# Scores of a quad: one addition of the bias over 512 columns and one reduction for the four maxima, in place of four fused operations

## The reference, cut to what matters

```python
q = jnp.einsum('bfd,dnh->bfnh', x, Wq) * H ** (-0.5)      # 16 heads of 64
k = jnp.einsum('btd,dnh->btnh', src, Wk)
v = jnp.einsum('btd,dnh->btnh', src, Wv)
hbias = jax.nn.relu(dist[..., None] @ Wth + bth)          # 32 hidden values for each (f, t)
qs_bias = (hbias @ Wto + bto)[..., 0]                     # one bias for each (b, f, t)
logits = jnp.einsum('btnh,bfnh->bnft', k, q)
logits = logits + bias + qs_bias[:, None]                 # the same bias for all 16 heads
w = jax.nn.softmax(logits, axis=-1)
out = jnp.einsum('bnft,btnh->bfnh', w, v)
```

## Time and profile before

| | us |
|---|---|
| median of 3 runs | 1346.33 (1345.58 to 1346.62) |
| profiled execution, its own time | 1342.64 |
| span of the profiled execution | 1340.6 |
| DVE busy | 1226.7 (92%) |
| PE busy / PEld busy | 1210.5 (90%) / 989.4 (74%) |
| ACT busy | 1062.0 (79%) |
| GpSimd busy | 852.6 (64%) |

### The profile page before, as it was taken

One profiled execution on the slowest core, in us unless ns is written; L12 is line 12 of the kernel. 1 busy time (PEld: TensorE's weight loads), 2 busy tenths in 40 slices (PEclk: granted clock), 3 DMA queues, 4 the chain that ended last, 5 costly groups with the idle time before them and its releaser, 6 DMA issues. The chain is left out here.

```text
span 1340.6 us, 36744 instructions
## 1 busy us (share of the span) xinstructions
PE 1210.5 (90%) x11184; PEld 989.4 (74%) x11184; DVE 1226.7 (92%) x4922; ACT 1062.0 (79%) x3353; POOL 852.6 (64%) x889
## 2 busy tenths in 40 slices
PE   1599999999999999999999999999999999789987
PEld 1377878787878787778777777778787878566665
DVE  5899999999999999999999999999999988579997
ACT  4588888888878888888888787878788866579887
POOL 4677777777777777777777777777777754211110
PEclk8799999999999999999999999999999999999999
DMA  6000000001100000011000000110000000000000
GB/s 189 17 1 17 2 17 2 18 17 49 35 15 4 10 10 9 10 56 43 2 17 2 17 2 17 49 43 10 17 2 25 2 2 3 1 10 13 14 16 9
DMA packets 32323, 26.69 MB, mean 20 GB/s; under 512 B 6649, under 2 KB 27009, under 8 KB 32129
## 3 DMA queue, kind: packets, MB, share of 16 engines
q1 hardware_dynamic: 32128, 24.35, 6.1%
HBM read 23.29 MB, written 1.05 MB: 18 GB/s over the span
## 5 line engine op out<-in xcount | busy, mean ns | idle before, releaser
L746 ACT ACTIVATE prob<-score,nmax 128x128 f32<-128x128 f32 x1024 | 397.0, 391 | 160.6 <-DVE nmax L941 160.6
L1341 POOL TENSOR_TENSOR prob<-prob,rinv 128x512 f32<-128x512 f32 x256 | 291.6, 1139 | 178.6 <-DVE rinv L949 178.1
L894 DVE SCALAR_TENSOR_TENSOR bias_acc<-relu_z,cst_all,bias_acc 128x512 f32<-128x512 f32 x370 | 349.2, 944 | 6.7 <-ACT relu_z L729 3.1
L729 ACT ACTIVATE relu_z<-dist_g,cst_all 128x512 f32<-128x512 f32 x386 | 295.7, 807 | 12.6 <-DMA dist_g<-in_fside_BxSxS 10.1
L941 DVE CUSTOM_DVE_ANT_0 score<-L,bias 128x128 f32<-128x128 f32 x1024 | 234.1, 281 | 2.9 <-PE L L472 1.6
L1336 POOL TENSOR_TENSOR sd<-mv,half 128x1 f32<-128x1 f32 x128 | 127.0, 992 | 120.6 <-DVE mv L963 119.4
L746 ACT ACTIVATION_READ_ACCUMULATOR prob<-score,nmax 128x1 f32 x1024 | 193.7, 189 | 0.0
L482 PE MATMUL T<-ident,prob 128*128 128x128 f32 x1024 | 160.5, 279 | 6.5 <-POOL prob L1341 4.2
L525 PE MATMUL M<-wv,ctxT_all 128*128 128x512 f32 x256 | 144.6, 647 | 18.5 <-DVE hid L1018 13.1
L496 PEld LDWEIGHTS O<-probT,v 128*64 128x64 f32 x2048 | 109.7, 136 | 59.8 <-issue 52.0
L472 PE MATMUL L<-kT,qT 64*128 64x128 f32 x2048 | 148.7, 285 | 0.0
(11 more groups left out here) (134 smaller groups left out, 2160.3 us busy)
## 6 DMA issues: line engine op xcount, KB each, us to landing
dist_g<-in_fside_BxSxS SPq DMA_DIRECT2D x16, 256.0 KB, 2.9
mask_g<-in_mask_Bx1x1xS_ff SPq DMA_DIRECT2D x16, 256.0 KB, 3.2
wk<-in_L_xattn_Wk SPq DMA_DIRECT2D x4, 512.0 KB, 3.5
wv<-in_L_xattn_Wv SPq DMA_DIRECT2D x4, 512.0 KB, 3.6
wq<-in_L_xattn_Wq SPq DMA_DIRECT2D x4, 512.0 KB, 3.7
wo<-in_L_xattn_Wo SPq DMA_DIRECT2D x4, 512.0 KB, 4.2
wf<-in_L_xattn_Wf SPq DMA_DIRECT2D x8, 256.0 KB, 2.9
xr<-in_x SPq DMA_DIRECT2D x16, 64.0 KB, 1.9
```

Of the source, the lines that this page charges most:

```text
L729: nc.scalar.activation(relu_z[:, z_slot(g, k), :], dist_g[:, :, :], ACT.Relu, bias=cst(g, C_BTH + k), scale=cst(g, C_WTH + k)).then_inc(z_ ...
L746: last = nc.scalar.activation(prob[:, c, m, :], score[:, c, m, :], ACT.Exp, bias=nmax[:, c, m:m + 1], scale=-1.0, accum_out=rsum[:, c, m:m ...
L894: vec.scalar_tensor_tensor(out=bias_acc[:, :], in0=relu_z[:, z_slot(g, k), :], scalar=weight, in1=bias_acc[:, :], op0=ALU.mult, op1=ALU.ad ...
L1341: gp.tensor_tensor(prob[:, c, :, :], prob[:, c, :, :], rinv[:, c, :].rearrange("p (m o) -> p m o", o=1).broadcast_to([P, 4, P]), ALU.mult) ...
```

## The change

`score_quad` now makes one addition over the 512 columns of the bank, with the unit's bias read four times over, raises a new semaphore `summed`, waits for it, and takes the four maxima (negated) in one reduction over `score`. `score` holds the sum itself instead of its negative, so the exponential has scale 1. PE waits for `summed` instead of `scored` before it overwrites the banks.

```diff
-                wait(pe, scored, after(g, i, 4, 2 * octet - 1))
+                wait(pe, summed, after(g, i, 4, 2 * octet - 1))
...
                     last = nc.scalar.activation(prob[:, c, m, :], score[:, c, m, :], ACT.Exp, bias=nmax[:, c, m:m + 1],
-                                                scale=-1.0, accum_out=rsum[:, c, m:m + 1])
+                                                scale=1.0, accum_out=rsum[:, c, m:m + 1])
...
-                for m in range(4):
-                    if m == 0:
-                        if i % GROUP == 0 and c == 0:
-                            dve.wait_ge(bias_done, g + i // GROUP + 1)
-
-                        wait_first(dve, consts, qk_done, after(g, i, 4, c), exp_done, after(g, i - 1, 4, c))
-                    last = vec.tensor_tensor_reduce(out=score[:, c, m, :], in0=L[c % 2][:, m * P:(m + 1) * P], in1=bias[:, i % GROUP, :],
-                                                    scale=-1.0, scalar=BIG, op0=ALU.add, op1=ALU.min,
-                                                    accum_out=nmax[:, c, m:m + 1])
-                last.then_inc(scored, 1)
+                if i % GROUP == 0 and c == 0:
+                    dve.wait_ge(bias_done, g + i // GROUP + 1)
+                wait_first(dve, consts, qk_done, after(g, i, 4, c), exp_done, after(g, i - 1, 4, c))
+                vec.tensor_tensor(score[:, c, :, :], L[c % 2][:, :].rearrange("p (m t) -> p m t", m=4),
+                                  bias[:, i % GROUP, :].rearrange("p (o t) -> p o t", o=1).broadcast_to([P, 4, P]),
+                                  ALU.add).then_inc(summed, 1)
+                dve.wait_ge(summed, after(g, i, 4, c))
+                vec.tensor_reduce(nmax[:, c, :], score[:, c, :, :], AX_X, ALU.max, negate=True).then_inc(scored, 1)
```

More of the change, by code:

```diff
@@ L245, in block_program @@
         qk_done, scored, exp_done, inv_done, normed = [sem(n) for n in ("qk_done", "scored", "exp_done", "inv_done", "normed")]
+        summed = sem("summed")
         pT_done = sem("pT_done")
```

## The result

| | before | changed |
|---|---|---|
| median of the runs | 1346.09 us (1345.58 to 1346.62) | 1419.67 us (1415.18 to 1420.29) |
| profiled execution | 1342.64 | 1415.18 |
| span | 1340.6 | 1413.3 |

The changed kernel is slower by 73.6 us, a ratio of 1.0539 with a 95% interval of 1.0519 to 1.0558. The forecast was +82 us, to 1428, with a range of 1403 to 1467.

The account below looks back on a forecast made before the run. DVE's own queue was taken as the bound: 256 x 0.485 = +124 us, less 27 absorbed behind quad 1, 10 before inverse 2 and 4 in the last units, rounded to +82: 1428 us. Range 1403 to 1467 (own case 1410 to 1446).

Parts of the forecast that it names:

- DVE's queue is the bound: Whole kernel: DVE's own queue limits while units have terms, busy 191.2 of 200 us.
- A quad of 1.33 us, +0.485: Each of 256 quads: addition 0.69, wait 0.04, reduction 0.60 us, against 0.84 before; +124 us if nothing gave way.
- The wait costs 0.04 us over an operation's full duration: Between a quad's addition and reduction: a 0.04 us gap, with 0.10 as high end and no cost as low end.
- The extra time of quad 1 is absorbed: Two terms behind quad 1: the first waits for GpSimd's add anyway, so 60 units give back 27 us.
- The wait in front of inverse 2 goes: DVE before inverse 2: a 0.16 us wait after quad 2's exponentials vanishes in 60 units, -10 us.
- Last four units: Units without terms: 7.8 us of extra quad time meet 12.6 idle us; half counted as absorbed, -4 us.
- Nothing absorbed: Rival, terms behind quad 1: their stretch is a price per term, so quad 1 costs full; runs 1466 us; chance 0.2.
- A free wait: Rival, each quad: reduction starts 0.61 us after the addition, quad 1.21 us, +0.36; runs 1404 us; chance 0.1.
- The reduction is not stretched: Denies the rival that GpSimd's clamp and add delay the reduction 1.5 us a unit: 1518 us; chance 0.03.
- The stretch did not dissolve: Denies the rival that stretch in quad 1's terms and L976 vanishes, -116 us: runs 1340, not slower; chance 0.03.

Follow-up runs that it names:

- Quad 1 alone: The kernel before with the new form (addition, wait, one reduction) in quad 1 of each unit only: 1344.80 us, ratio 1.0001.
- the cut kernel before: The kernel before with GpSimd's product, clamp and add on one column, leaving out 8 of 32 bias terms: 1325.76 us, ratio 0.9866.
- the gap-filled kernel: The changed kernel with one DVE operation between each quad's addition and reduction: 1454.60 us, ratio 1.0818 to the kernel before.

## Why the prediction was right, point by point

- *DVE's queue is the bound.* Right: DVE's share stays, PE's and ACT's fall, and PE's wait for summed is worth nothing. It holds for a change that lengthens DVE's queue. Shortened by 67 us in its terms, the same queue made the kernel only 17 us faster, since ACT was next.
- *A quad of 1.33 us, +0.485.* Measured 1.32 and +0.477 in the mean of 16.
- *The wait costs 0.04 us over an operation's full duration.* Right: with an operation between, addition and reduction add 0.60 each, and a quad is 0.13 us shorter (18.98 against 21.12 for 16). The Trainium skill (VectorE: DVE Perf Modes, The DRAIN you can't avoid) says of a chain of copies that the semaphores between them cost nothing extra. The runs differ: a semaphore between two DVE operations is not free here. The prediction gives that section by half: it also says that a next operation which is not held starts earlier, and with that the 0.61 us from start to start agrees.
- *The extra time of quad 1 is absorbed.* Right. Quad 1 alone costs 0.0 us (interval -2 to +2), and all terms together gave back 26.9 us in the 15 groups, where 27 were forecast.
- *The wait in front of inverse 2 goes.* Right: 0.36 to 0.20 in three units of a group, and in the fourth 0.57 to 0.20, which one unit could not show: 12 us where 10 were forecast.
- *Last four units.* +4 forecast, by counting half of 7.8 without a row for the half; 3.9 measured. That it fits so well is luck in part.
- *The size:* 82 forecast, 73.6 measured. In 60 units it was 79 against 71: 3 us less in the quads, nothing in the terms, 2 in front of inverse 2, and 3 in small distances (inverses, copies) which I had taken as fixed.
- *Rivals.* Nothing absorbed (+120) is refuted by quad 1 alone. A free wait (+58) is refuted by the reduction's start at 665.19 behind an addition that ends at 665.16. The reduction is not stretched: 685 to 689 ns in all 256. The reason given against that rival was thin: the earlier trace rows have two lines, L891 and L976, that read one tensor from SBUF and are stretched, so that reading SBUF alone was no safeguard. The stretch did not dissolve; and where it was made to, in the cut kernel before, ACT's waits kept three quarters of it. So that case could not have become faster by the sum that I gave for it: it left out what is late next.

## What to carry to other kernels

Working over more columns at once is no gain if it splits one pass into two: here four fused operations over 128 columns with their accumulator reads (0.84 us) beat two operations over 512 (1.32). Price such an edit place by place, by what stands behind each copy of it: here the same 0.48 us cost from 0 to 29 us in a run, depending on whether a wait for another engine followed, and on which operation releases that engine. Before moving an operation to fill a gap, look at whom it releases.

## What the runs showed of the hardware

- A DVE operation with two SBUF inputs (the terms) that starts while a GpSimd operation over 512 columns is in progress ends 0.53 to 0.55 us after that one's end, wherever it started: in 158 cases before, in 131 changed, and in the gap-filled kernel alike. One that starts in the last 0.14 us of it takes its usual 0.75. Alone it takes 0.71 to 0.75. The other way round GpSimd is stretched too: in the kernel before its norm takes 1.03 to 1.05 us in 194 cases, and 1.42 to 1.51 in the 62 in which it starts while a term runs. The runs show the times and that the order matters, not what is shared. The Trainium skill (SBUF — State Buffer, SBUF: two separate sides) names it: a pair of ports for which a DVE operation with two SBUF inputs and a GpSimd operation that reads SBUF contend, as an exclusive lock that is held for the whole instruction. That whichever starts second is the one that is stretched agrees with it. That a term ends 0.53 to 0.55 and not 0.71 behind GpSimd's end, as if its first 0.2 us had passed during the wait, is not explained by any run.
- The addition (one input from PSUM, one from SBUF) and the reduction (one from SBUF) are not stretched beside the same GpSimd work: 659 to 692 ns and 685 to 689 in all 256 quads. This does not hold for every operation with one SBUF input: L976, a subtraction and a multiplication over 128 columns, takes 0.35 us with GpSimd idle and in 57 units of the kernel before 0.67, where it starts while GpSimd's norm runs; and the first term of a group, L891, has a median of 1.24 us where its least is 0.55.
- Reading the bias four times over through a repeated dimension shows no cost: 681 ns against 693 for a plain addition of 512 columns. That one has both inputs in SBUF, so it is the nearest row and not the same operation without the repeat.
